# Layer two in units of 4 and 4 steps, the first unit routed inside turns 6 and 7 of attention

## The reference

```python
x = x + 0.5 * ffn(layernorm(x))          # layer one
x = x + attention(layernorm(x))          # 16 heads, chunks of 128 tokens, a carried state
x = x + 0.5 * ffn(layernorm(x))          # layer two, same weights

def ffn(xf):
    logits = xf @ Wr.T + br              # 8 experts
    e = argmax(logits, axis=-1)          # one expert for each token
    h = relu(W1[e] @ xf + b1[e])         # 128 -> 512
    return W2[e] @ h + b2[e]             # 512 -> 128
```

## Time and profile before

| what | value |
|---|---|
| median of 3 runs | 430.17 us (429.95 to 430.38) |
| profiled execution, its own time | 426.96 us |
| its span, first to last instruction | 424.9 us |
| mean granted TensorE clock | 0.909 of full speed |
| busy: PE, DVE, ACT, POOL | 358.1, 288.4, 192.1, 284.5 us |
| indirect DMAs of GpSimd: gathers, scatters | 92 of 955 ns, 46 of 1002 ns |

### The profile page before, as it was taken

How to read it: one execution, slowest core, us unless ns; L and a number is a source line. 1 busy time by engine, 2 the same in 40 slices (tenths; PEclk the granted TensorE clock), 3 DMA queues, 4 the chain that set the end, 5 groups by cost and what they waited for, 6 DMA issues and landing times.

```text
span 424.9 us, 10262 instructions
## 1 busy us (share of the span) xinstructions
PE 358.1 (84%) x2508; PEld 319.2 (75%) x2508; DVE 288.4 (68%) x995; ACT 192.1 (45%) x608; POOL 284.5 (67%) x303
## 2 busy tenths in 40 slices
PE   6788989999989979879897978855589999999920
PEld 6787879999978767667676766645489899999910
DVE  4872675444563698999898989897665676566510
ACT  5723745565546322535456363240455435555500
POOL 0027774754885999998989777620777777777770
PEclk9555999999999979998999999986599999999975
DMA  8938686887761000001010110102687846767410
GB/s 231 349 107 270 194 240 186 223 190 231 219 188 41 21 0 19 2 19 57 7 62 2 50 49 2 50 2 71 191 238 246 199 139 193 228 198 199 134 35 0
DMA packets 41303, 54.00 MB, mean 127 GB/s; under 512 B 6212, under 2 KB 25818, under 8 KB 40992
## 3 DMA queue, kind: packets, MB, share of 16 engines
q1 hardware_dynamic: 34640, 39.97, 29.9%
q0 software_dynamic: 6176, 13.26, 13.0%
q10 hardware_dynamic: 432, 0.14, 0.2%
HBM read 41.93 MB, written 12.32 MB: 128 GB/s over the span
## 4 chain that ended last, share of the span: by engine, by line
PE 55%; POOL 15%; DVE 11%; issue 10%; ACT 3%; DMA 2%; DVEq 1%; POOLq 0%; ACTq 0%
PE bank L1226 17%; PE bank L1216 17%; POOL outer_all L451 5%; PE bank L1272 4%; POOL rows L410 4%; PE bank L1176 4%; PE bank L1170 3%; POOL qS L459 3%; PE bank L1254 3%; PE bank L1208 2%; PE bank L1192 2%; POOL out_x L429 2%; PE bank L1290 2%; DVE st L702 1%; POOL kd L438 1%
## 5 line engine op out<-in xcount | busy, mean ns | idle before, releaser
L396 POOL DMA_INDIRECT ring<-rows_d,token_in x92 | 87.8, 955 | 78.0 <-DVE token_in L884 50.9
L1216 PE MATMUL bank<-slot_xT,w_ring 128*128 128x128 f32 x736 | 103.9, 283 | 4.9 <-DVE hT_b L924 4.0
L1216 PEld LDWEIGHTS bank<-slot_xT,w_ring 128*128 128x128 f32 x736 | 93.6, 197 | 8.6 <-DVE hT_b L924 6.0
L924 DVE TENSOR_SCALAR hT_b<-bank,b_cur 128x128 f32<-128x128 f32 x184 | 56.0, 346 | 38.2 <-PE bank L1216 32.6
L451 POOL TENSOR_TENSOR outer_all<-qkv 128x512 f32<-128x512 f32 x64 | 66.4, 1063 | 4.0 <-ACT qkv L577 4.0
L1272 PE MATMUL bank<-outer_all,decay_sb 128*128 128x256 f32 x256 | 68.0, 392 | 1.0 <-DVE qS L966 1.0
L560 ACT ACTIVATE hT_a<-bank,b_cur 128x128 f32<-128x128 f32 x184 | 57.3, 363 | 12.4 <-PE bank L1216 11.5
L1226 PE MATMUL bank<-w_sb,hT_a 128*128 x368 | 59.2, 284 | 3.4 <-DVE ring L937 0.6
L1272 PEld LDWEIGHTS bank<-outer_all,decay_sb 128*128 128x128 f32 x256 | 48.3, 197 | 16.6 <-issue 5.4
L1226 PE MATMUL bank<-w_sb,hT_b 128*128 x368 | 56.5, 276 | 0.0
L429 POOL DMA_INDIRECT out_x<-ring,token_out x46 | 46.1, 1002 | 14.0 <-issue 11.9
(11 more groups left out here) (127 smaller groups left out, 498.8 us busy)
## 6 DMA issues: line engine op xcount, KB each, us to landing
w_ring<-in_w1t SPq DMA_DIRECT2D x92, 256.0 KB
rows_d<-rows SPq DMA_DIRECT2D x8, 512.0 KB, 2.9
y_d<-kd SPq DMA_DIRECT2D x46, 64.0 KB
rows<-in_x SPq DMA_DIRECT2D x8, 256.0 KB, 5.9
w_sb<-in_w2t SPq DMA_DIRECT2D x1, 2048.0 KB, 8.8
rows_d<-rows SPq DMA_DIRECT2D x8, 256.0 KB, 3.7
ring<-rows_d,token_in POOLq DMA_INDIRECT x92, 4.0
decay_sb<-in_decay SPq DMA_DIRECT2D x1, 1024.0 KB, 8.1
```

What stands on the lines that cost most here:

```text
L396: pool.indirect_dma_start(n_in_ring(G) if layer_of(G) == 0 else in_ring(G), None, rows_d[u], bass.IndirectOffsetOnAxis(ap=token_in[u][:, j ...
L924: last = nc.vector.tensor_scalar(hT_b[G % 2][:, f * P:(f + 1) * P], bank_b[:, f * P:(f + 1) * P], b1_cur[G % 2][:, 2 + f:3 + f], 0.0, ALU. ...
L1216: last = mm(to[:, f * P:(f + 1) * P], w1_ring[G % W1_BUFS][:, (2 * half + f) * P:(2 * half + f + 1) * P], slot_xT[G % 2][:, :], start=True ...
```

## The change

Layer two is split (4, 4): two units of 16 tiles and 23 slots. The router works on raw residual rows, as layer one does: logit = rstd * (x W) + shift * (sum of W) + bias, put together on VectorE (`shift_logits`, `scale_logits`). So `route_transpose` needs only the residual (`res_done`) and moves one turn up: turn k routes step k-2. ScalarE keeps norms and raw products (`keep_norms`, `keep_logits`); `router_bias` goes. The tables of unit 2 move out of `outer[0]` into buffers that are idle then (`hT_a`, `hT_b`, `w1_ring`), its counts into bank 7 and its inverse into bank 4. VectorE builds the table between the operations of turn 6, and reads it in turn 7; three gathers go into turn 7. What stood behind turn 7 (statistics and small operations of turn 8) moves into hooks 0 to 3 of layer two's pass; the other hooks move up to four slots later. SP waits for the inverse before it loads W1 for layer two. The core of the diff:

```diff
-SPLIT = ((5, 3), (5, 3))
+SPLIT = ((5, 3), (4, 4))
-        EARLY_RESULTS, GATHERS_FIRST = 17, 6
+        EARLY_RESULTS, GATHERS_FIRST = 14, 4
+        in_weights = [t[:, :] for t in (*hT_a, *hT_b)] + [w1_all[:, :]]
+        table = [lay_out(u, *(in_weights if u == MID_UNIT else [in_outer])) for u in range(UNITS)]
+        counts_bank = [bank[7] if u == MID_UNIT else bank[5] for u in range(UNITS)]
+        placed_bank = [bank[4] if u == MID_UNIT else bank[5] for u in range(UNITS)]
...
@@ SP
-            for s in range(STEPS - 2):
+            for s in range(STEPS - 3):
                 store_rows(1, s)
-            loads(LAYER_TILES, LAYERS * LAYER_TILES, {2: lambda: store_rows(1, 6), 5: lambda: store_rows(1, 7)})
+            sp.wait_ge(placed_ready[MID_UNIT], 1)
+            loads(LAYER_TILES, LAYERS * LAYER_TILES, {-1: lambda: store_rows(1, 5), 7: lambda: store_rows(1, 6),
+                                                      12: lambda: store_rows(1, 7)})
...
@@ GpSimd, attention(n); ahead(n, 1) gathers one slot where n is the last turn
                 half_sum(n, 3)
+                ahead(n, 1)
                 half_sum(n, 4)
+                ahead(n, 1)
...
+                ahead(n, 1)
                 half_sum(n, 6)
...
-            gather(UNIT[2].start, UNIT[3].start)
+            gather(gathered[0], UNIT[3].start)
...
@@ ScalarE
+            def keep_norms(k):
+                act.wait_ge(ln_ready, ln_turn(k) + 1)
+                first = (k - 2) * BATCH
+                for dst, src in ((rstd_all, rstd[k % 2]), (shift_all, shift[k % 2])):
+                    last = nc.scalar.activation(dst[:, first:first + BATCH], src[:, ROUTED:ROUTED + BATCH], ACT.Copy)
+                last.then_inc(norms_kept, 1)
+
+            def keep_logits(n):
+                act.wait_ge(logits_ready, STEPS + n + 1)
+                w = BATCH * EXPERTS
+                nc.scalar.activation(logits[:, n * w:(n + 1) * w], bank[4][:, 0:w], ACT.Copy).then_inc(logits_kept, 1)
...
-                if 0 <= k - 3:
-                    route_copy(STEPS + k - 3, step(k - 3).par, bank[4])
+                if 0 <= k - 2:
+                    route_copy(STEPS + k - 2, step(k - 2).par, bank[4])
...
                     normalise_output(k)
+                if 0 <= k - 2:
+                    keep_norms(k)
+                    keep_logits(k - 2)
...
             expert_pass(1, {
-                0: lambda: normalise_output(8), 1: lambda: (output_copy(8), route_copy(STEPS + 5, 1, bank[4])),
-                2: lambda: normalise_routed(8), 4: lambda: route_copy(STEPS + 6, 0, bank[4]),
-                5: lambda: normalise_routed(9), 7: lambda: route_copy(STEPS + 7, 1, bank[4])})
+                2: lambda: route_copy(STEPS + 6, 0, bank[4]), 4: lambda: normalise_output(8),
+                5: lambda: (output_copy(8), keep_norms(8), keep_logits(6)), 6: lambda: normalise_routed(8),
+                9: lambda: route_copy(STEPS + 7, 1, bank[4]), 10: lambda: (keep_norms(9), keep_logits(7)),
+                11: lambda: normalise_routed(9)})
...
@@ VectorE; (k, h) is a place ahead of sum_d(k, h)
+            between = {(6, 0): lambda: (shift_logits(2), scale_logits(2)), (6, 1): lambda: (route_best(2), route_prefer(2)),
+                       (6, 2): lambda: route_onehot(2), (6, 4): lambda: route_count(2),
+                       (6, 5): lambda: (route_rank(2), route_place(2)), (6, 6): lambda: (invert_slots(2), invert_ids(2)),
+                       (6, 7): lambda: invert_lanes(2), (7, 0): lambda: route_owners(2), (7, 2): lambda: invert_read(2)}
             for k in TURNS:
                 attention(k)
-                if k == ROUTE_TURN:
...
             expert_pass(1, {
-                2: lambda: (gate(step(7)), router_bias(5)),
-                3: lambda: (residual_stats(9), turn_small(9, 0, 4, ROUTED, ROUTED + BATCH)),
-                4: lambda: turn_small(9, 4, SMALL + 1, ROUTED, ROUTED + BATCH), 5: lambda: router_bias(6),
-                8: lambda: (router_bias(7), route_best(3)), 9: lambda: route_prefer(3), 10: lambda: route_onehot(3),
-                11: lambda: route_count(3), 12: lambda: route_rank(3),
-                13: lambda: route_place(3), 14: lambda: (invert_slots(3), invert_ids(3)),
-                15: lambda: invert_lanes(3), 16: lambda: route_owners(3), 17: lambda: invert_read(3)})
+                0: lambda: residual_stats(8), 1: lambda: turn_small(8, 0, 5, *both), 2: lambda: turn_small(8, 5, 9, *both),
+                3: lambda: turn_small(8, 9, SMALL + 1, *both), 5: lambda: gate(step(7)),
+                7: lambda: (residual_stats(9), last_small(0, 3)()), 8: last_small(3, 8), 9: last_small(8, SMALL + 1),
+                11: lambda: (shift_logits(3), scale_logits(3)), 12: lambda: (route_best(3), route_prefer(3), route_onehot(3)),
+                13: lambda: route_count(3), 14: lambda: (route_rank(3), route_place(3)),
+                15: lambda: (invert_slots(3), invert_ids(3)), 16: lambda: invert_lanes(3), 17: lambda: route_owners(3),
+                18: lambda: invert_read(3)})
...
@@ TensorE
             def route_transpose(s):
-                pe.wait_ge(rows_kept, STEPS + s.n + 1)
-                wait(pe, logits_added, s.n)
-                transpose4(bank[4], lambda b: n_of(s.n * BATCH + b), rnT_ready)
+                pe.wait_ge(res_done, s.n + 1)
+                wait(pe, logits_kept, s.n)
+                if s.n == 5:
+                    pe.wait_ge(ends_known, 1)
+                transpose4(bank[4], lambda b: x_of(s.n * BATCH + b), rnT_ready)
...
+                    if k == 6:
+                        pe.wait_ge(counts_read[MID_UNIT], 1)
                     inter_product(cur)
...
+            between = {(6, 5): count_mid, (7, 1): invert_mid}
...
             expert_pass(1, {
-                0: lambda: out_transpose(step(7)), 1: lambda: route(5), 2: lambda: out_product(step(7)),
-                3: lambda: route_transpose(step(6)), 4: lambda: route(6), 6: lambda: route_transpose(step(7)),
-                7: lambda: route(7), 10: lambda: route_counts(3), 16: lambda: invert(3)})
+                0: lambda: out_product(step(6)), 1: lambda: route_transpose(step(6)), 3: lambda: route(6),
+                4: lambda: out_transpose(step(7)), 6: lambda: out_product(step(7)), 8: lambda: route_transpose(step(7)),
+                9: lambda: route(7), 12: lambda: route_counts(3), 16: lambda: invert(3)})
```

More of the change, by code:

```diff
@@ L79 @@
 BIAS_W = FF + D
+MID_UNIT = GROUPS
 def step(k):
@@ L122, in build @@
         ring = sb("ring", [P, RING * ROW])
-        w1_ring = [sb(f"w1_ring{i}", [P, FF]) for i in range(W1_BUFS)]
+        w1_all = sb("w1_all", [P, W1_BUFS * FF])
+        w1_ring = [w1_all[:, i * FF:(i + 1) * FF] for i in range(W1_BUFS)]
         w2_sb = sb("w2_sb", [P, EXPERTS * FF])
@@ L164, in build, with lay_out @@
         logits = sb("logits", [P, TOKEN_TILES * EXPERTS])
[L165 to L177, removed]
+        Tables = namedtuple("Tables", "upto place onehot_bf ended in_slot in_slot_id in_lane")
+        def lay_out(u, *parts):
+            tiles, slots, ways = UNIT[u].tiles, UNIT[u].slots, 2 if u < GROUPS else 3
+            sizes = ((tiles * EXPERTS, F32), (tiles * EXPERTS, F32), (tiles * EXPERTS, BF16), (slots * EXPERTS, F32),
+                     (tiles * slots, BF16), (tiles * ways * slots, BF16), (tiles * P, BF16))
+            at, tables = [0] * len(parts), []
+            for width, dt in sizes:
+                size = width if dt == F32 else (width + 1) // 2
+                i = next(i for i in range(len(parts)) if at[i] + size <= parts[i].shape[1])
+                view = parts[i][:, at[i]:at[i] + size]
+                tables.append(view if dt == F32 else view.bitcast(dt))
+                at[i] += size
+            return Tables(*tables)
+        in_outer = outer[0]
+        in_weights = [t[:, :] for t in (*hT_a, *hT_b)] + [w1_all[:, :]]
+        table = [lay_out(u, *(in_weights if u == MID_UNIT else [in_outer])) for u in range(UNITS)]
         best = sb("best", [P, MAX_TILES])
@@ L465, in fetch_one, with ahead @@
                 fetch_back(s, b, b + 1)
+            gathered = [UNIT[2].start]
+            def ahead(n, count):
+                if n == STEPS - 1:
+                    gather(gathered[0], gathered[0] + count)
+                    gathered[0] += count
             def attention(n):
@@ L759, in route_norms @@
                     small(i, 0, UNIT[g].tiles, g, ln_chain0[g], 0, ln_chain0[g])
[L761 to L766, removed]
             chains = [Chain(dve, route_chain[u]) for u in range(UNITS)]
             counts_of = lambda u: UNIT[u].tiles * EXPERTS
+            norms_of = lambda u, layer1, layer2: (layer1[u][:, 0:UNIT[u].tiles] if u < GROUPS else
+                                                  layer2[:, UNIT[u].first:UNIT[u].first + UNIT[u].tiles])
             by_tile = lambda t: t.rearrange("p (i e) -> p i e", e=EXPERTS)
@@ L857, in invert_slots @@
```

(8 more changed lines are left out.)

122 lines of the change are left out of this document (55 added, 67 removed).

## The result

445.36 us median (442.95 to 445.93, four runs) against 430.06 for the kernel before on the same chip (429.39 to 430.38): ratio 1.0358, 95% interval 1.0316 to 1.0399, so 15.3 us slower. The forecast was slower by 9, at 439, with a range to 446.

What follows compares the result with a forecast made beforehand. GpSimd's DMA queue was taken as the bound from the seam on: unit 3's table at 298.5 + 55 = 353.5, plus 80.45, ends the span at 433.9, 9.0 over 424.9; added to the 430.17 median, 439 us, range 431 to 446.

Steps and rivals of the forecast that it cites:

- T: When unit 3's table is ready in layer two's pass: forecast 353.5, with the span ending 80.45 us behind it.
- S: Start of layer two's pass, its first up product: forecast 298.5, where it was 302.67 before.
- L: Time from the start of layer two's pass to unit 3's table: forecast 54.95 us, before 46.75.
- Turn 6, and blocking: Attention turn 6: 7.45 us of added VectorE work, plus 1.6 for VectorE and GpSimd blocking each other over SBUF.
- Turn 7: Attention turn 7: the owners and the table's read add 1.9 us on VectorE.
- L, hook 0: Hook 0 of the pass: step 6's residual waits for an output product, 0 to 2.1 us, taken as 0.7.
- L, the hooks: VectorE's added hook work in layer two's pass costs 5.6 us, and reading the table one hook later 1.9.
- What GpSimd does until T: GpSimd's queue ahead of unit 3's first gather: one idle time of 10 to 20 us, then 55 issues without a gap.
- Hooks hidden behind TensorE: Rival for layer two's pass: VectorE's hooks fit into TensorE's time, table at 338, time 423.7 us; chance 0.10.
- Nothing measurable: Rival: unit 3's table between 343.5 and 345.5, so no measurable change, 431.3 us at the least harm; chance 0.04.
- The loads in turn 7: Rival: three gathers don't begin in turn 7; GpSimd has 18 us to spare, forecast time unchanged; chance within the forecast's 0.66.
- Blocking to its end: Rival in turn 6: VectorE and GpSimd block fully, pass starts at 303, time 443.8 us; chance 0.16.

Runs made afterwards that it cites:

- the two comparisons above: The changed kernel's slot results and granted clock held against those of residual later (442.04 us) and of thin outer products (441.2 us).
- thin outer products: Changed kernel with GpSimd's eight outer products of step 7 replaced by multiplications of 8 columns: 441.2 us; same edit on the kernel before: 427.2 us.
- residual later: Changed kernel with step 6's residual and statistics, `residual_stats(8)`, moved from hook 0 to hook 1 of layer two's pass: 442.04 us.

## Why the prediction was right about the sign and 6 us short

The frame held: the end is T plus the issues behind it. Forecast 80.45 from T to the end, measured 80.8; T was forecast at 353.5 and came at 360.05 on that scale, outside the 347 to 358 that I gave for it. The 6.5 us are S (298.5, came at 302.5) and L (54.95, came to 57.6).

- **Turn 6, and blocking: the step that failed.** I took 7.45 of work and 1.6 of blocking; the turn grew by 12.3. Eight operations of turn 6 are 4.9 longer in sum than in the pass, and 7.45 + 4.9 is 12.35: the work was sized rightly, the blocking was not. Five of the eight stand beside the six outer products and are 3.24 longer in sum. That is near the 3.1 "if each has to wait", of which I took half, and no row spoke for the half. The other three, 1.65 longer, stand beside half sums and `kd`, which I had not counted. The Trainium skill, SBUF — State Buffer, section Who interferes with whom, says of a VectorE operation with two inputs from SBUF and a GpSimd instruction that reads SBUF that the later one blocks until the other is through; the trace agrees (the scan of `ends_e`, both inputs from SBUF, took 0.99 for 0.22 beside products of 1.04).
- **Turn 7.** 1.9 was forecast, 3.16 came: one blocked operation of the owners (0.87 for 0.33) and two waits for TensorE, 0.18 and 0.53. Turns 1 to 5 added 0.4 (forecast 0.3), `shift` to S took 5.3 (5.9). The matmuls, copies and gathers costed at nothing cost no more than that.
- **L, hook 0.** Taken as 0.7, with an upper end of 2.1, by the output product alone. The residual also stands ahead of slot 0's own work, and VectorE waited 4.01 for it; the first result came 8.98 behind S instead of 5.71, 3.3 later.
- **L, the clock.** Not in the sum at all: 2.4 by the two comparisons above, though no run changed the clock alone.
- **L, the hooks.** Forecast 5.6 and 1.9 for one hook later; what is left of the growth of 10.8 is 10.8 - 3.3 - 2.4 = 5.1 (not measured on its own), so 2.4 too much. Three errors of L partly cancel, and that the time lies within the range, 0.6 below its end, is luck: with 5.1 for the hooks the forecast would have been 436.8 and the range would have ended at 443.6.
- **What GpSimd does until T.** I expected one idle time of 10 to 20 ahead of the gather. It stands 18.6 in all, but 7.6 of it there; the rest is ahead of six scatters. Early scatters are no free filler, since their results come from the same slowed pass. With 17 of them the last result is 1.6 us late for the gather, and with 14 the time is still 2.45 longer.
- **The rivals.** Hooks hidden behind TensorE: T - S would have been 41, it was 57.6, and hooks two slots later cost two slots. Nothing measurable fell with it. The loads in turn 7 were worth nothing, as said, since GpSimd stood 18.6 us ahead of T. Blocking to its end, 443.8 at 0.16, is what came nearest, with S at 303; I gave the middle too much.

## What to carry to other kernels

Where one engine works off a fixed queue, price a change by the queue's last wait: what must be there, when, and how many issues stand behind it; a shift of work that makes an earlier queue entry ready buys nothing if that last wait moves the other way. Work that fills a stretch in which nobody is the bound (here VectorE in the seam) is free where it is; moved into the stages on both sides, it is paid almost in full (in turn 6, 7.4 of the 8.65 that I had added up, blocking left aside). And before interleaving small VectorE operations with GpSimd's, ask for each whether all its operands lie in SBUF. Here such operations took up to the length of GpSimd's instruction instead of their own, all but the reductions, which kept theirs.

## What the runs showed of the hardware that I had not expected

Blocking is not confined to operations with two inputs from SBUF: a TENSOR_SCALAR of 128x8 with one, from SBUF to SBUF, went from 0.17 to 0.99 beside GpSimd's products. It doesn't hold for all with one such input either: the TENSOR_REDUCE of the state products, from SBUF to SBUF too, kept its 0.59 (0.59 alone in before). Operations that read one operand from PSUM beside the same products kept their length (the two of `route_rank`, 0.28 and 0.29). VectorE's timeline of after:

```profile
272.70 0.59 DVE L1010 TENSOR_REDUCE o_in<-qS 128x64 f32<-128x256 f32 x1
...
274.63 0.28 DVE L868 TENSOR_TENSOR hT_a<-bank,hT_a 128x128 f32<-128x128 f32 x1
```

GpSimd's own six took 6.25 against 6.20 before, so nearly all of it falls on VectorE. GpSimd's DMA issues in layer two's pass held up little: in before, the TENSOR_SCALAR and the scan of 128x8 took 0.17 beside one. But a TENSOR_SCALAR of 128x368 in bf16 took 0.50 beside a scatter's issue, and 0.31 away from one (VectorE and GpSimd of after, then VectorE with the hooks two later):

```profile
355.31 0.50 DVE L904 TENSOR_SCALAR outer_all<-outer_all,const_sb 128x368 bf16<-128x368 bf16 x1
```

```profile
354.75 0.98 POOL L437 DMA_INDIRECT out_x<-ring,token_out  x1 [1.16 <-DVE ring L972]
```

```profile
358.76 0.31 DVE L904 TENSOR_SCALAR outer_all<-outer_all,const_sb 128x368 bf16<-128x368 bf16 x1
```

The granted clock fell behind an idle gap: where TensorE idled 1.62 to 1.76 us near S + 5, it went to 1.2 GHz for about 3.4 us soon after, and again 20 us later (the kernel after, the two with other early scatters or later hooks, and 4 and 4 steps with the table in turn 7); in kernels with the gap at 1.33 (thin outer products) and 1.15 (residual later) it stayed at 2.4 GHz, and T - S was 55.0 and 54.4 instead of 57.6. That is a correlation over these traces: no run changed the clock alone, and what brings the second fall is open.

A granted clock of 1.00 in the profile has to be held against the matmuls. In the trace of after it stands at 1.00 from 7 to 40 us, and yet the first up product of layer one takes 2.07 at 37.13, as in before, whose clock is 0.50 there, and as long as at S (2.08 at 0.50). So the mean clocks of whole traces, 0.909 before and 0.941 after, can't be compared. The falls in the pass are borne out by the matmuls, 25 of them in 4 us.
